# The first microseconds of a two-product adapter kernel: TensorE multiplies zeros while the batches are sorted, and the first role's weights come in fewer, wider transfers

## The reference

```python
# x [128, 128, 1024], role [128] in {1, 2}; W_down [3, 1024, 512], W_up [3, 512, 1024]
h = jnp.einsum('bsh,bhk->bsk', x, W_down[role]) + b_down[role][:, None, :]
h = jax.nn.gelu(h, approximate=False)
u = jnp.einsum('bsk,bkh->bsh', h, W_up[role]) + b_up[role][:, None, :]
y = x + u
mean, var = mean and variance of y over the 1024 features
out = (y - mean) * rsqrt(var + 1e-5) * gamma[role][:, None, :] + beta[role][:, None, :]
```

## Time and profile before

| what | value |
|---|---|
| median of three runs | 1424.94 us |
| the profiled execution | 1425.9 us, its span 1424.0 us |
| TensorE busy with matmuls | 1405.2 us, 99% |
| VectorE, ScalarE, GpSimd busy | 1206.0, 779.2, 188.0 us |
| mean granted TensorE clock | 0.998 |
| moved by DMA | 283.52 MB, 199 GB/s |

### The profile page before, as it was taken

The page is one execution under the profiler, slowest core; times in us unless marked ns, Lnnn a source line. Parts: engine busy times, 40 slices in busy tenths (PEclk is TensorE's granted clock), DMA queues, the critical chain, the costliest instruction groups (busy, mean ns, idle before and its releaser), DMA issues.

```text
span 1424.0 us, 32330 instructions
## 1 busy us (share of the span) xinstructions
PE 1405.2 (99%) x6175; PEld 1158.7 (81%) x6176; DVE 1206.0 (85%) x1454; ACT 779.2 (55%) x2059; POOL 188.0 (13%) x297
## 2 busy tenths in 40 slices
PE   8999999999999999999999999999999999999997
PEld 6878888888888888888888888888888888888886
DVE  7789988788888888888888899888888888888888
ACT  5555555555555555555555555555555555555555
POOL 4367311100000000000000376311100000000000
PEclk9999999999999999999999999999999999999999
DMA  9678777866665665666566777777765666566563
GB/s 220 185 219 232 204 205 196 221 185 198 203 185 186 199 204 181 195 198 193 182 200 199 211 224 234 219 202 206 199 214 181 197 198 190 184 195 204 183 195 138
DMA packets 208726, 283.52 MB, mean 199 GB/s; under 512 B 25775, under 2 KB 155312, under 8 KB 208702
## 3 DMA queue, kind: packets, MB, share of 16 engines
q1 hardware_dynamic: 201726, 269.60, 61.6%
q0 software_dynamic: 5888, 12.07, 4.8%
q10 hardware_dynamic: 1088, 1.57, 0.4%
HBM read 183.27 MB, written 99.88 MB: 199 GB/s over the span
## 4 chain that ended last, share of the span: by engine, by line
PE 87%; DVE 6%; DVEq 4%; issue 3%; ACT 1%; DMA 0%; ACTq 0%; SPq 0%
PE p_down L989 14%; PE p_down L991 14%; PE p_down L990 14%; PE p_up L989 14%; PE p_up L991 14%; PE p_up L990 14%; DVEq L241 3%; DVE row L744 1%; DVE row L798 1%; DVE row L737 1%; DVE hT_lo L730 1%; DVE xT_raw L714 1%; DVE h L758 0%; DVE row L768 0%; DVE xT_lo L718 0%
## 5 line engine op out<-in xcount | busy, mean ns | idle before, releaser
L989 PE MATMUL p_up<-wu_hi,hT_hi 128*128 x1008 | 393.3, 390 | 2.9 <-DVE hT_lo L730 2.6
L989 PE MATMUL p_down<-wd_hi,xT_hi 128*128 x1012 | 394.3, 390 | 0.0
L990 PE MATMUL p_down<-wd_lo,xT_hi 128*128 x1012 | 393.9, 389 | 0.0
L991 PE MATMUL p_down<-wd_hi,xT_lo 128*128 x1012 | 393.7, 389 | 0.0
L991 PE MATMUL p_up<-wu_hi,hT_lo 128*128 x1008 | 392.2, 389 | 0.0
L990 PE MATMUL p_up<-wu_lo,hT_hi 128*128 x1008 | 392.2, 389 | 0.0
L559 ACT ACTIVATE hT_hi<-p_hT 128x512 fp32r<-128x512 f32 x126 | 75.5, 599 | 401.4 <-DVE p_hT L724 399.2
L744 DVE SCALAR_TENSOR_TENSOR row<-p_up,row 128x1024 f32<-128x1024 f32 x126 | 154.2, 1224 | 153.8 <-PE p_up L991 143.5
L545 ACT ACTIVATE xT_hi<-xT_raw 128x1024 fp32r<-128x1024 f32 x125 | 132.8, 1062 | 174.7 <-PE p_down L991 116.9
L989 PEld LDWEIGHTS p_up<-wu_hi,hT_hi 128*128 128x128 f32 x1008 | 188.9, 187 | 45.5 <-issue 6.6
L989 PEld LDWEIGHTS p_down<-wd_hi,xT_hi 128*128 128x128 f32 x1012 | 190.3, 188 | 40.7 <-issue 1.1
(11 more groups left out here) (164 smaller groups left out, 951.2 us busy)
## 6 DMA issues: line engine op xcount, KB each, us to landing
x_quad<-in_x SPq DMA_DIRECT2D x510, 128.0 KB, 3.5
row<-in_x SPq DMA_DIRECT2D x126, 512.0 KB, 4.0
out<-row SPq DMA_DIRECT2D x126, 512.0 KB, 2.8
h_dram<-h SPq DMA_DIRECT2D x125, 256.0 KB, 4.0
h_quad<-h_dram SPq DMA_DIRECT2D x500, 64.0 KB, 2.0
w_raw<-in_L_cond_W_down POOLq DMA_DIRECT2D x64, 64.0 KB, 3.6
w_raw<-in_L_cond_W_up POOLq DMA_DIRECT2D x64, 64.0 KB, 3.0
row<-in_L_cond_W_up SPq DMA_DIRECT2D x16, 128.0 KB, 5.3
```

The costliest lines, as they stand in the source:

```text
L989: pe.matmul(dst, a_hi, w_hi, start=first, stop=False)
L990: pe.matmul(dst, a_hi, w_lo, start=False, stop=False)
L991: return pe.matmul(dst, a_lo, w_hi, start=False, stop=last)
```

## The change

Three things are changed in the head; the steady loop is untouched.

1. GpSimd clears half of `xT_lo` (128x512). `keep_clock` multiplies these zeros rather than rounded weights: five matmuls before the keys are spread, two before the order matmul, three before the `spread` matmuls, and after these two, a wait for the first turned half of x, and two more. The last raises `zeros_used`, and VectorE waits for it before it writes the first half of batch 0 into `xT_lo`.
2. A piece of the first role's weights comes by transfers whose destination is all 128 partitions: one for each chunk c of W_down (256 KiB, two for a piece), one for a whole W_up piece (512 KiB).
3. ScalarE's queue takes pieces 0, 1 and the first chunk of piece 2 ahead of x; the second half-load on ScalarE after the first rounding is gone. SyncE's takes the second chunk of piece 2 and piece 3 after x of batch 1.

```diff
+        zeros_ready, zeros_used = sem("zeros_ready"), sem("zeros_used")
+        wd_chunk = W_down.rearrange("r (q c a) k -> r c q a k", q=NQ, a=BLK)
+        wu_chunk = W_up.rearrange("r (q c a) h -> r c q a h", q=NQ, a=BLK)
-        def load_first(eng, n, quads=range(NQ)):
-            buf = row[n % RING]
-            for q in quads:
-                if n < FD:
-                    w = FC // K
-                    dst = buf[BLK * q:BLK * q + BLK, 0:FC].rearrange("p (c k) -> p c k", c=w)
-                    eng.dma_start(dst, wd_view[R - 1, q, :, n * w:n * w + w, :]).then_inc(first_raw[n], 16)
-                else:
-                    eng.dma_start(buf[BLK * q:BLK * q + BLK, 0:FC], wu_view[R - 1, q, :, n - FD, :]).then_inc(
-                        first_raw[n], 16)
+        def load_first_down(eng, n, c):
+            at = c * K
+            eng.dma_start(row[n % RING][:, at:at + K], wd_chunk[R - 1, n * (FC // K) + c]).then_inc(first_raw[n], 16)
+        def load_first_up(eng, n):
+            eng.dma_start(row[n % RING][:, 0:FC], wu_chunk[R - 1, n - FD]).then_inc(first_raw[n], 16)
...
-            load_first(sp, FD - 2, range(NQ // 2, NQ))
-            load_first(sp, FD - 1)
+            load_first_down(sp, FD - 2, 1)
+            for c in range(FC // K):
+                load_first_down(sp, FD - 1, c)
...
-                load_first(sp, n)
+                load_first_up(sp, n)
...
+            pool.memset(xT_lo[:, 0:HALF, :].bitcast(F32), 0.0).then_inc(zeros_ready, 1)
...
-            load_first(act, 0, range(0, 1))
+            load_first_down(act, 0, 0)
             act.wait_ge(out_ready, 1)
             act.activation(factor[:, 0:1], opener[:, 2:3], ACT.Gelu)
-            load_first(act, 0, range(1, NQ))
-            load_first(act, 1)
+            for n, c in ((0, 1), (1, 0), (1, 1), (2, 0)):
+                load_first_down(act, n, c)
...
             round_first(0)
-            load_first(act, FD - 2, range(0, NQ // 2))
...
+                if (b, half) == (0, 0):
+                    dve.wait_ge(zeros_used, 1)
...
         @block.tensor
+            def keep_clock(count):
+                for _ in range(count):
+                    mm = pe.matmul(p_down[:, :], xT_lo[:, 0, :], xT_lo[:, 0:HALF, :], start=True, stop=True)
+                return mm
+
+            pe.wait_ge(zeros_ready, 1)
+            keep_clock(5)
             pe.wait_ge(key_ready, 1)
             pe.matmul(p_up[0][:, 0:B], ones_row, key, start=True, stop=True)
             pe.matmul(p_up[0][:, B:B + 1], key, ones_row[:, 0:1], start=True, stop=True).then_inc(key_spread, 1)
+            keep_clock(2)
             pe.wait_ge(order_ready, 1)
...
-            pe.wait_ge(first_hi, 1)
-            keep_clock(2)
+            keep_clock(3)
             pe.wait_ge(ident_ready, 2)
...
-            keep_clock(4)
+            keep_clock(2)
+            pe.wait_ge(half_turned, 1)
+            keep_clock(2).then_inc(zeros_used, 1)
             pe.wait_ge(first_known, 2)
```

More of the change, by code:

```diff
@@ L437, in load_params @@
                     pool.wait_ge(loaded, 16 * part + 16)
-            raw_once = 16 * NQ
-            pool.wait_ge(first_raw[FD + FU - 1], raw_once)
+            pool.wait_ge(first_raw[FD + FU - 1], 16)
             pool.wait_ge(numbers_ready, 1)
@@ L500, in first_piece @@
             buf = row[n % RING][:, 0:FC]
-            count = 16 * NQ
             if n < FD:
-                return buf, wd_hi[:, n * FC:n * FC + FC], wd_lo[:, n * FC:n * FC + FC], count
+                return buf, wd_hi[:, n * FC:n * FC + FC], wd_lo[:, n * FC:n * FC + FC], 16 * (FC // K)
             m = n - FD
-            return buf, wu_hi[:, m * FC:m * FC + FC], wu_lo[:, m * FC:m * FC + FC], count
+            return buf, wu_hi[:, m * FC:m * FC + FC], wu_lo[:, m * FC:m * FC + FC], 16
         @block.scalar
         def _(act):
-            load_first(act, 0, range(0, 1))
+            load_first_down(act, 0, 0)
             act.wait_ge(out_ready, 1)
             act.activation(factor[:, 0:1], opener[:, 2:3], ACT.Gelu)
-            load_first(act, 0, range(1, NQ))
-            load_first(act, 1)
+            for n, c in ((0, 1), (1, 0), (1, 1), (2, 0)):
+                load_first_down(act, n, c)
             act.wait_ge(first_known, 1)
@@ L956, in spread @@
                 return pe.matmul(dst, pick, rows, start=True, stop=True)
-            def keep_clock(count):
-                for _ in range(count):
-                    pe.matmul(p_down[:, :], wd_hi[:, 0:P], wd_hi[:, 0:K], start=True, stop=True)
-            pe.wait_ge(first_hi, 1)
-            keep_clock(2)
+            keep_clock(3)
             pe.wait_ge(ident_ready, 2)
```

## The result

The changed kernel takes 1454.95 us (median of 5 runs, 1453.2 to 1455.18) against 1424.94 of the kernel before (5 runs). By the medians that is 30.0 us slower; the time forecast was 1454.5. The ratio, taken from the runs and not from the two medians, is 1.0206, interval 1.0193 to 1.0219. The profiled execution took 1455.0, with a span of 1453.3.

A forecast was written before the change was run, and what follows sets the result against it. TensorE's stream, busy 99%, was taken as the bound. Weights on four engines would delay batch 3's first matmul by 28.6 us, plus 1 for the clock restart: +29.6 on the median, 1454.5 us, range 1423 to 1468.

The forecast's parts named there:

- Four engines: First role's weight transfers: four source blocks against 128 partitions run on four of 16 DMA engines; chance 0.76 with faster engines.
- The rate: Weight transfers in the head: one DMA engine moves 20 kB/us, bounds 16 to 24.
- T, the last piece: Landing of the last W_up piece: 2 + 1147/20 + 1 for the landing = 60.4 us.
- the sum: Head's transfers: start at 2 us, 1147 kB per engine at 20 kB/us, 1 us landing, giving 60.4 us.
- the likeliest case's range: Whole kernel, if the weight transfers run on four engines: 1443 to 1468 us.
- Behind T: After the last W_up piece: x of batch 3 lands, is processed, first matmul 5.5 us later; clock restart costs 1 more.
- Part 1, the zeros: Head's fillers on cleared zeros: if the clock rises by 8.5 us, first product at 12.3, 1.8 us earlier.
- Rival A: New weight transfers use all 16 engines and fillers warm the clock: -1.2 us, 1423.7; chance 0.18.
- rival B: All 16 engines, but zeros don't raise the clock early and their series eats the gain: 0 to +1 us; chance 0.06.
- My series of zeros, subtraction and product: Ahead of batch 0's first product: last zeros, 0.69 us subtraction and product follow in series; product at 12.3 warm, 13.9 cold.
- Part 3, the order: Queue order of W_down pieces and x loads in the head: costs or gains under 1 us where transfers use 16 engines.

The follow-up runs named there:

- c16: Changed kernel, but each new weight transfer's source is 128 consecutive rows instead of four blocks of 32 (output not the reference's): 1424.90 us, ratio 1.0007.
- c8: Changed kernel, but each new weight transfer's source is eight blocks of 16 rows instead of four of 32 (output not the reference's): 1434.38 us, ratio 1.0071.
- c2: Changed kernel, but each new weight transfer's source is two blocks of 64 rows instead of four of 32 (output not the reference's): 1493.58 us, one run only.
- b2: Kernel before with only the four W_up pieces as one transfer of 128 partitions each: 1438.39 us, ratio 1.0106.
- w1: b2, but SyncE waits for the last W_up piece to land before it issues x of batch 3: 1438.45 us, ratio 1.0104.
- z4: z3 with TensorE's three register loads of weight positions moved ahead of the last two parameter spreads: 1424.14 us, ratio 1.0004.
- a1: Changed kernel with its zeros and issue order kept, but the first role's weights by the old transfers of 32 partitions: 1426.14 us, ratio 1.0016.
- z1: Kernel before plus only the clearing, the fillers on zeros and VectorE's wait; transfers and queue order as before: 1423.76 us, ratio 0.9994.
- z3: z2 with all of W_down piece 2 on SyncE's queue behind x of batch 1: 1423.88 us, ratio 0.9994.
- z2: z1 with the zeros in hT_lo and VectorE's wait moved to batch 1's subtraction: 1424.59 us, ratio 1.0006.

## Why the prediction was right, step by step

The mechanism is the forecast one, and the experiments show it. That the time came within 0.5 us of the number is luck, as follows.

**Four engines.** Right, and shown by c16, c8 and c2: the inference from closing packets (16 for each transfer of 32 rows, one for each small row) held for a source of 4 outer blocks against 128 partitions.

**The rate.** This term was mis-sized. I took 20 kB/us from the fast stage of the earlier trace rows, where sixteen engines at once had shown 20.7; the weights alone ran at 24.7 to 26.3, over the upper bound (24).

**T, the last piece.** Forecast 60.4; ScalarE rounds it at 60.54, from the timeline of the kernel after:

```profile
28.18 1.30 DVE L699 STREAM_TRANSPOSE xT_raw<-x_quad 128x512 f32<-128x512 f32 x2 [12.58 <-DMA x_quad<-in_x]
...
31.48 0.79 PE L995 MATMUL p_down<-wd_hi,xT_hi 128*128 x1 [1.30 <-DVE xT_lo L707]
...
31.53 5.94 SPq L261 DMA_DIRECT2D row<-in_L_cond_W_up  x4
...
53.09 1.06 ACT L522 ACTIVATE wu_hi<-row 128x1024 fp32r<-128x1024 f32 x1 [4.12 <-DMA row<-in_L_cond_W_up]
...
60.54 1.06 ACT L522 ACTIVATE wu_hi<-row 128x1024 fp32r<-128x1024 f32 x1 [6.39 <-DMA row<-in_L_cond_W_up]
```

That is right by errors that cancel. At the true rate the sum would have given T = 2 + 1147/24.7 + 1 = 49.4, and a time near 1443.5, at the lower end of the likeliest case's range. The other 11 us are time in which the four engines did not run at that rate, and which the sum had nothing for. The trace of the kernel after has them in three parts of about 5, 3 and 5 us; the sum's 1 us for the landing and its 1.3 for x of batch 2 lie in these too. Four stretches between (columns as in the earlier trace rows):

```profile
28.00:30.00 2.00, 1.05 (x2) 0.50 (x2) 1.30 (x2) 1.07 (x2) 0.00 (x0) 1.00 0.26 100
30.00:32.00 2.00, 0.70 (x2) 0.50 (x2) 1.79 (x3) 1.55 (x3) 0.00 (x0) 1.00 0.58 173
32.00:34.00 2.00, 2.00 (x6) 1.54 (x5) 1.87 (x5) 1.31 (x2) 0.00 (x0) 1.00 0.55 147
34.00:36.00 2.00, 2.00 (x6) 1.52 (x6) 2.00 (x4) 1.22 (x2) 0.00 (x0) 1.00 0.23 72
```

- From 2 to about 31 us W_down and x of batches 0 and 1 (524 + 66 kB for each engine) took 29 us, where that rate makes 23.9. From 2 to 4 us the queues moved only 46 GB/s; the rest of the 5 us lies between 7 and 16 us, among the loads of x, and is not taken apart.
- From 31 to 35 us the weights nearly stood. The queues moved 590 kB, of which x of batch 2 is 524, so W_up got under 100 kB where four engines move 99 in each microsecond. SyncE asked for W_up only at 31.53: it had stood 11.6 us ahead of x of batch 2, whose buffer comes free with batch 0's transpose at 28.18, and W_up is queued behind it. W_down, asked for earlier, ran on meanwhile, so of the 11.6 us only this lull is lost. The step named x of batch 0 at 25 to 30 us, but not who stands behind it on SyncE.
- From 35 to 60.54 us the rest of W_up took 25.5 us, where that rate makes 20.3. Its last pieces came 6.8 and 7.45 us apart and not 131/24.7 = 5.3, while x of batches 3 and 4 and a row of x moved.

b2 and w1 show the last of the three by experiment, in the kernel of before; the others are read from the trace of after.

**Behind T.** Forecast 5.5 us by way of x of batch 3, with the piece's own rounding, split and matmuls beside it, and 1 for the clock. x did land 1.1 us behind the piece (61.66), but the path was the other one: batch 3's x was subtracted by 64.03 + 1.23 = 65.26, and the piece's own path was the later one, because VectorE transposed x first (61.66 + 1.25) and split the piece after it. Then six W_up matmuls and the first of batch 3 ran 0.43 us apart, after a stretch with the granted clock at 0.50 (above). Six at 0.43 are 2.6 us where 1.4 was put. The two together: 66.84 - 60.54 = 6.3, forecast 6.5.

**The rest.** Share 0.27 for 0.25, 99 GB/s for 80, first product 31.48 for "about 30", last split 62.83 for 62, batch 3 at 66.84 for 66. The first rounding was at 13.29, not 9: ScalarE itself was stuck issuing (below).

**Part 1, the zeros.** Clearing took 0.51 us in the timeline (0.4 to 0.9 forecast). The fillers ran from 2.17 us, and in the kernels whose weights use 16 engines they brought the 0.23 us spacing earlier than in the kernel before, which had it at 14.7; but it came only between 9.4 and 12 us, and 8.5 was wrong in every kernel. Rival A's -1.2 us did not come: c16, which is rival A's transfer, came out at +0.07%, as rival B had it. My series of zeros, subtraction and product also lacked a term: I priced what queues behind the new wait on VectorE, and not what queues behind the one on TensorE. z4 puts about 1.2 us on its three register loads. None of it shows in the time of the change, where batch 0 comes at 28 us anyway.

**Part 3, the order.** "Under 1 us" was wrong for the old transfers: -0.8 was counted, a1 shows +2 against z1. I had looked at batch 1's x only, and not at batch 0's, ahead of which the piece was put. With wide transfers on 16 engines (c16) the same order has batch 3 at 37.32, and no such loss is seen.

No version beat the kernel before by more than can be measured; z1 and z3 are nearest, at 0.9994.

## What to carry to other kernels

Before merging small transfers into a large one, look at the outermost count of both access patterns and not at the partitions or bytes: closing packets in the queue's count tell how many engines a transfer uses, and with few of them the rate falls nearly in proportion (99 GB/s on 4, 51 on 2). Where a wait is added, price what is queued behind it on every engine that waits, register loads too. And when the predicted sum comes out, compare its terms: here a rate set too low by a fifth hid 11 us of lulls and slowed pieces.

## What the hardware showed that I had not expected

**Issuing stalls when few engines are backed up.** The queue's own instructions in the timeline of the kernel after, and one in b2:

```profile
7.42 5.82 ACTq L267 DMA_DIRECT2D x_quad<-in_x  x2
...
13.29 1.06 ACT L522 ACTIVATE wd_hi<-row 128x1024 fp32r<-128x1024 f32 x1 [9.74 <-issue]
```

```profile
22.73 9.18 SPq L272 DMA_DIRECT2D x_quad<-in_x  x4
```

Two issues held ScalarE's sequencer for 5.82 us, and with it the first rounding; one transfer of W_down took 2.06 to issue in the kernel after, and in b2 four loads of x held SyncE for 9.18, where four issued later without that backlog took 1.81. A busy queue is thus a wait for the engine that issues, not for the data alone. Why is not shown.

**Small loads suffer with them.** The parameter loads are 1 or 2 rows and so run on one or two engines. VectorE takes the last of them at 10.42 us in the kernel after and at 8.95 in c8, at 7.21 in the kernel before and at 7.19 in c16, whose weights are on all 16. That the weights queue on the very engines of these rows fits this, but the traces don't name the engines. From the kernel after:

```profile
10.42 0.71 DVE L846 CAST wu_hi<-h 103x512 fp32r<-103x512 f32 x1 [3.19 <-DMA h<-in_L_cond_b_up]
```

**Register loads are dear.** Three loads on TensorE's sequencer were worth 1.25 us in z4. The Trainium skill, DMA: Bandwidth & Descriptors, section Latency and other measured facts, gives a floor of about 600 ns for a `tensor_load`. If the register loads here are that, three would take 1.8 us at least, an estimate by that page. In z3 they stood in the 2.58 us between the turned half and the first product, which leaves room for it, and moving them gave 1.25; a single one has no duration in these traces.

**The clock.** The kernels with zeros all ran 2.5 us of fillers from 2.17 us and had gaps of some tenths after them. Yet TensorE reached the 0.23 us spacing at about 9.4 us in z4, 10.2 in z2 and z3, 11.1 in z1 and 12 in a1 and c16, and not before 17 us in after and c8. And a stand of 1.8 us cost a1 three microseconds at the lower level, while one of 1.5 us cost z1 and one of 1.7 us cost z3 none. What decides it stays open.
